# Where the four-bit weights of the last feed-forward stages are quantised: a stage of their own, or spread over rope attention

## The reference

```python
def fp4_quant_dequant(x):                       # blocks of 16 along the last dimension
    scale = max(abs(block)) / 6.0               # at least 1e-12
    idx = searchsorted(_MID, abs(block / scale))  # grid 0, .5, 1, 1.5, 2, 3, 4, 6
    return _GRID[idx] * sign(block) * scale
gate = fp4_linear(x, w_gate); y = fp4_linear(x, w_up)     # 352 x 128 each
return fp4_linear(silu(gate) * y, w_down)                 # 128 x 352
```

## Time and profile before

| | |
|---|---|
| Runs | 2240.65, 2242.89, 2244.3 us |
| Span of the profiled execution | 2239.6 us |
| Median of the runs less that span | 3.3 us |
| DVE busy | 1683.9 us, 75% |
| PE busy | 1850.4 us, 83% |
| POOL busy | 1024.6 us, 46% |

### The profile page before, as it was taken

The page is one execution under the profiler, slowest core; times in us unless marked ns, Lnnn a source line. Parts: engine busy times, 40 slices in busy tenths (PEclk is TensorE's granted clock), DMA queues, the critical chain, the costliest instruction groups (busy, mean ns, idle before and its releaser), DMA issues. The chain is left out here.

```text
span 2239.6 us, 35939 instructions
## 1 busy us (share of the span) xinstructions
PE 1850.4 (83%) x11864; PEld 1449.0 (65%) x11895; DVE 1683.9 (75%) x4329; ACT 1171.2 (52%) x2207; POOL 1024.6 (46%) x904
## 2 busy tenths in 40 slices
PE   4888877968888799957997997997994679999856
PEld 3666664746666677735775885765883467777734
DVE  7899975879899787766777775676677856777787
ACT  3777753237777565524555553334553245666332
POOL 4898951238998655502654762002662421111022
PEclk9999998979999989977998998998996879999978
DMA  3000000000000033305432431002440010000000
GB/s 123 1 1 1 1 12 1 3 1 1 1 1 1 1 105 119 100 5 124 130 117 52 133 125 59 1 0 67 135 128 6 0 49 1 2 1 2 1 0 20
DMA packets 57189, 91.49 MB, mean 41 GB/s; under 512 B 8664, under 2 KB 19736, under 8 KB 56880
## 3 DMA queue, kind: packets, MB, share of 16 engines
q1 hardware_dynamic: 57008, 89.25, 13.6%
HBM read 87.34 MB, written 1.88 MB: 40 GB/s over the span
## 5 line engine op out<-in xcount | busy, mean ns | idle before, releaser
L1041 POOL TENSOR_TENSOR unit_hid_low<-unit_hid,unit_hid_high 128x512 fp32r<-128x512 f32 x272 | 352.9, 1298 | 280.6 <-ACT unit_hid_high L1217 280.3
L800 DVE SCALAR_TENSOR_TENSOR pk_chosen<-bank,pk_least,pk_sums 128x1024 f32<-128x1024 f32 x256 | 325.6, 1274 | 44.4 <-issue 37.2
L665 ACT COPY pk_sums<-bank 128x1024 f32<-128x1024 f32 x256 | 261.2, 1021 | 123.3 <-PE bank L563 122.9
L563 PE MATMUL bank<-pk_pick,pk_sim_both 128*128 128x512 f32 x512 | 190.1, 453 | 106.6 <-DVE pk_chosen L800 106.6
L479 POOL TENSOR_TENSOR pk_chosen<-pk_chosen 128x1024 f32<-128x1024 f32 (+1 forms) x126 | 265.5, 2110 | 13.6 <-DVE pk_chosen L800 13.6
L1098 PE MATMUL bank<-unit_x_high,units_high 128*128 128x512 f32 x544 | 222.4, 409 | 19.4 <-ACT unit_gact L1210 8.3
L1099 PE MATMUL bank<-unit_x_low,units_high 128*128 128x512 f32 x544 | 218.0, 401 | 0.0
L1100 PE MATMUL bank<-unit_x_high,units_low 128*128 128x512 f32 x544 | 217.8, 400 | 0.0
L1217 ACT CAST unit_hid_high<-unit_hid 128x512 fp32r<-128x512 f32 x272 | 166.7, 613 | 55.6 <-DVE unit_hid L1364 27.8
L563 PEld LDWEIGHTS bank<-pk_pick,pk_sim_both 128*128 128x128 f32 x512 | 78.6, 192 | 165.1 <-DVE pk_chosen L800 128.5
L1210 ACT ACTIVATE unit_gact<-bank,units_small 128x512 f32<-128x512 f32 x136 | 93.7, 689 | 104.8 <-PE bank L1100 102.7
(11 more groups left out here) (404 smaller groups left out, 4456.3 us busy)
## 6 DMA issues: line engine op xcount, KB each, us to landing
unit_comb<-comb_dram SPq DMA_DIRECT2D x136, 256.0 KB, 3.2
unit_comb<-comb_dram SPq DMA_DIRECT2D x272, 128.0 KB, 3.1
raw<-in_geglu_units SPq DMA_DIRECT2D x3, 774.0 KB, 6.9
raw<-in_swiglu_units SPq DMA_DIRECT2D x3, 768.0 KB, 9.7
dh_w<-in_de_w SPq DMA_DIRECT2D x1, 1024.0 KB, 6.0
out_x<-x_res SPq DMA_DIRECT2D x1, 1024.0 KB, 5.1
raw<-in_geglu_units SPq DMA_DIRECT2D x1, 967.5 KB, 10.3
raw<-in_swiglu_units SPq DMA_DIRECT2D x1, 960.0 KB, 12.4
```

What stands on the lines that cost most here:

```text
L563: ins = nc.tensor.matmul(sums_ps[:, 2 * b + e, :], both[:, i % 2, h, :], pk.pick[:, e * PK_K // 2:(e + 1) * PK_K // 2, :].rearrange("p i j ...
L665: nc.scalar.copy(sums_sb[:, b, :].rearrange("p (e n) -> p e n", e=2), sums_ps[:, 2 * b:2 * b + 2, :]).then_inc(sums_out.sem, 1)
L800: nc.vector.scalar_tensor_tensor(chosen[:, h, :].rearrange("p (e n) -> p e n", e=2), sums_ps[:, 2 * b:2 * b + 2, :], least2[:, i % 2, h:h ...
L1041: nc.gpsimd.tensor_tensor(hid_low[:, i % HB, :], hid[:, i % HB, :], hid_high[:, i % HB, :].bitcast(FP32), ALU.subtract).then_inc(hidden.se ...
```

## The change

- `program`: the seven loads are issued by the first `experts_ffn` of the third layer instead of the second. `f4.quantise()` and its block are gone; `rope_attention` gets `f4`.
- Two counters are added, `f4_cleared` and `f4_scaled`.
- DVE, ahead of the loop of rope attention: `find_scales`, the scales and their reciprocals of `rows` and `cols`, interleaved (8 instructions), behind a wait for the loads and for POOL's clearing.
- POOL, ahead of its set-up: the clearing and a drain. Behind its loop: `round`, nine instructions for each of the two tensors. It does not take the step from the exponent bits; it compares the square with 4 and 16 instead.
- PE, behind its loop: `turn`, the nine transposes. ACT, behind its loop: `read_turned`, the five copies.

```diff
@@ rope_attention
+        f4.scratch(ctx)
         @block.gpsimd
         def _(pool):
+            f4.clear(pool)
+            nc.gpsimd.drain()
             nc.gpsimd.memset(zeros[:], 0.0)
...
                 nc.gpsimd.tensor_copy(xb[:], k.xnT[:, bass.ts(b, T)]).then_inc(x_in.sem, 1)
+            f4.round(pool)
...
+            f4.turn(pe)
...
+            f4.read_turned(act)
...
         def _(dve):
+            f4.find_scales(dve)
             dve.wait_ge(loaded.sem, loaded.at(80))
             with dve.Fori(0, B) as b:
...
+    f4.passed()
@@ Fp4Weights
-    def quantise(self):
...
+    def clear(self, pool):
+        self.k.nc.gpsimd.memset(self.rows[F4_CHUNKS[2][1]:P, :, 2, :], 0.0).then_inc(self.k.counter("f4_cleared").sem, 1)
+    def find_scales(self, dve):
+        dve.wait_ge(loaded.sem, loaded.at(16 * 7))
+        dve.wait_ge(cleared.sem, cleared.at(1))
+        for f, w in self.parts:
+            nc.vector.tensor_reduce(f.scale[:], blocked(w), axis=AX.X, op=ALU.max, apply_absolute_value=True)
+        nc.vector.drain()
+        for f, w in self.parts:
+            nc.vector.tensor_scalar(f.scale[:], f.scale[:], 1.0 / F4_MAX, F4_SCALE_MIN, ALU.mult, ALU.max)
+        nc.vector.drain()
+        for f, w in self.parts:
+            nc.vector.reciprocal(f.inv[:], f.scale[:])
+        nc.vector.drain()
+        for f, w in self.parts:
+            nc.vector.tensor_scalar_mul(f.inv[:], f.inv[:], F4_TIES_DOWN).then_inc(scaled.sem, 1)
+    def round(self, pool):
+        pool.wait_ge(scaled.sem, scaled.at(2))
+        for f, w in self.parts:
+            near, step = f.near[:], f.step[:].bitcast(FP32)
+            nc.gpsimd.tensor_tensor(blocked(near), blocked(w), over(f.inv[:]), ALU.mult)
+            nc.gpsimd.drain()
+            nc.gpsimd.tensor_tensor(w, near, near, ALU.mult)
+            nc.gpsimd.drain()
+            nc.gpsimd.tensor_scalar(step, w, 4.0, F4_ROUND, ALU.is_ge, ALU.mult)
+            nc.gpsimd.tensor_scalar(w, w, 16.0, 2.0 * F4_ROUND, ALU.is_ge, ALU.mult)
+            nc.gpsimd.drain()
+            nc.gpsimd.tensor_tensor(step, step, w, ALU.add)
+            nc.gpsimd.drain()
+            nc.gpsimd.tensor_scalar(step, step, F4_ROUND, None, ALU.add)
+            nc.gpsimd.drain()
+            nc.gpsimd.tensor_tensor(near, near, step, ALU.add)
+            nc.gpsimd.drain()
+            nc.gpsimd.tensor_tensor(near, near, step, ALU.subtract)
+            nc.gpsimd.drain()
+            nc.gpsimd.tensor_tensor(blocked(w), blocked(near), over(f.scale[:]), ALU.mult).then_inc(rounded.sem, 1)
+    def turn(self, pe):
+        pe.wait_ge(rounded.sem, rounded.at(2))
...
+    def read_turned(self, act):
+        act.wait_ge(turned.sem, turned.at(1))
...
@@ program
-                experts_ffn(k, ew)
-                rope_attention(k, a)
-                experts_ffn(k, ew, f4.load)
-        f4.quantise()
+                experts_ffn(k, ew, f4.load)
+                rope_attention(k, a, f4)
+                experts_ffn(k, ew)
```

More of the change, by code:

```diff
@@ L68 @@
     comb_in_0 comb_in_1 comb_in_2 comb_in_3 comb_in_4
-    loaded set_up f4_loaded f4_rounded f4_turned dh_loaded
+    loaded set_up f4_loaded f4_cleared f4_scaled f4_rounded f4_turned dh_loaded
     x_in
@@ L2058, with rope_attention @@
 ROPE_BASE = 10000.0
-def rope_attention(k, a):
+def rope_attention(k, a, f4):
     nc = k.nc
@@ new lines, in scratch @@
+    def scratch(self, ctx):
+        self.f_rows, self.f_cols = Fp4Scratch(self.k, ctx, 6 * P), Fp4Scratch(self.k, ctx, F4_I)
+        self.parts = ((self.f_rows, self.rows[:].rearrange("p i c d -> p (i c d)")), (self.f_cols, self.cols[:]))
+    def clear(self, pool):
+        self.k.nc.gpsimd.memset(self.rows[F4_CHUNKS[2][1]:P, :, 2, :], 0.0).then_inc(self.k.counter("f4_cleared").sem, 1)
+    def find_scales(self, dve):
+        nc, loaded, cleared, scaled = self.k.nc, self.loaded, self.k.counter("f4_cleared"), self.k.counter("f4_scaled")
+        dve.wait_ge(loaded.sem, loaded.at(16 * 7))
[11 more added lines that the diff above has]
+            nc.vector.tensor_scalar_mul(f.inv[:], f.inv[:], F4_TIES_DOWN).then_inc(scaled.sem, 1)
@@ new lines, in round @@
+    def round(self, pool):
+        nc, scaled, rounded = self.k.nc, self.k.counter("f4_scaled"), self.k.counter("f4_rounded")
+        pool.wait_ge(scaled.sem, scaled.at(2))
[17 more added lines that the diff above has]
+            nc.gpsimd.tensor_tensor(blocked(w), blocked(near), over(f.scale[:]), ALU.mult).then_inc(rounded.sem, 1)
@@ new lines, in turn @@
+    def turn(self, pe):
+        k, nc, rounded, turned = self.k, self.k.nc, self.k.counter("f4_rounded"), self.k.counter("f4_turned")
+        pe.wait_ge(rounded.sem, rounded.at(2))
+        for i in range(2):
+            for c, (at, n) in enumerate(F4_CHUNKS):
+                nc.tensor.transpose(k.bank[i][:, at:at + n], self.rows[0:n, i, c, :], k.ident[0:n, 0:n])
+        for c, (at, n) in enumerate(F4_CHUNKS):
+            ins = nc.tensor.transpose(k.bank[2][0:n, c * P:(c + 1) * P], self.cols[:, at:at + n], k.ident[:])
+        ins.then_inc(turned.sem, 1)
@@ new lines, in read_turned, with passed @@
+    def read_turned(self, act):
+        k, nc, turned = self.k, self.k.nc, self.k.counter("f4_turned")
+        act.wait_ge(turned.sem, turned.at(1))
+        for i in range(2):
+            nc.scalar.copy(self.up[:, i, :], k.bank[i][:, 0:F4_I])
+        for c, (at, n) in enumerate(F4_CHUNKS):
+            nc.scalar.copy(self.down[0:n, c, :], k.bank[2][0:n, c * P:(c + 1) * P])
+    def passed(self):
+        self.loaded.passed(16 * 7)
+        for name, n in (("f4_cleared", 1), ("f4_scaled", 2), ("f4_rounded", 2), ("f4_turned", 1)):
+            self.k.counter(name).passed(n)
```

## The result

| | before | after | ratio, 95% interval |
|---|---|---|---|
| Median of the runs | 2241.77 us (4 runs, 2240.58 to 2244.3) | 2228.3 us (4 runs, 2227.78 to 2232.16) | 0.9943 (0.9928 to 0.9958) |
| The same comparison again, E11 | 2243.59 us (11 runs, 2235.78 to 2247.05) | 2231.41 us (6 runs, 2230.54 to 2233.92) | 0.995 (0.9936 to 0.9965) |

A forecast was written before the change was run, and what follows sets the result against it. No engine was taken as full; the serial quantising stage lay wholly on the path. -16.1 (stage) + 1.2 (rotation) + 3.9 (one-element holds) + 2.0 (tail) = -9.0 us, to 2233.9 us, range 2228.5 to 2239.0.

The forecast's parts named there:

- The stage goes: Between second expert stage and the next: the quantising stage's 16.4 us shrink to a 0.32 us passage, -16.1 us.
- Scales and loads: Scales ahead of VectorE's rope attention loop, loads in the first expert stage: both covered, 0 us, scales with 1.2 to spare.
- Rounding on GpSimd: Behind GpSimd's rope attention set-up: lasts 20.5 us, off the path with over 100 us of cover.
- upper price: GpSimd's tensor-scalars priced like plain two-input instructions, 2.39 ns per column, so the rounding lasts 25 us.
- the 5.9 at which the change would have lost: Slower case: GpSimd's compares at 5.9 ns per column make VectorE's waits lose the remaining 9.0 us; chance 0.03.
- The last rotation: First pass of rope attention: VectorE's last rotation is held by GpSimd's first product, +1.2 us, or 0.
- The one-element L2285: VectorE's one-element scaling before each exponential is held by GpSimd's reads: 5.9 us, +3.9 after absorbing, ends 0 and 11.
- The first rival: One-element instructions are free; only the last rotation and one or two joins are held: -12.2 us, 2230.7; chance 0.28.
- Transposes and copies: At the end of rope attention, uncovered: nine transposes and five copies add 2.0 us, bounds 1.3 and 3.0.
- no slower than before: The stage after the removed quantising stage starts earlier and keeps its length, TensorE's clock having been at 0.50 already: 0.

The follow-up runs named there:

- E11: The changed kernel itself once more, measured beside two later runs: 2231.41 us, 0.995 against the kernel before.
- E7: The kernel before with only the seven loads moved from the second to the first expert stage: 2242.75 us, 1.0008.
- E4: The changed kernel with the negated row maximum made for two elements per partition in place of one: 2231.98 us, 0.9962.
- E1: The changed kernel with GpSimd's rounding left out, weights used unrounded: 2229.12 us, 0.9952 against the kernel before.
- E8: The changed kernel with the scales found three times over on VectorE ahead of its loop: 2232.99 us, 0.9964.
- E2: The changed kernel with 24 GpSimd memsets, which only write, in place of the rounding: 2230.61 us, 0.9954.
- E5: The changed kernel with GpSimd waiting for the first pass's six rotations before it starts rounding: 2231.07 us, 0.9954.
- E9: The changed kernel with 24 drains on VectorE ahead of the scales, shifting its loop's code: 2228.99 us, 0.9937.
- E6: The changed kernel with the transposes and copies moved into the first four-bit feed-forward stage: 2232.6 us, 0.9961.

## Why the prediction was right, and where it was not

*The stage goes:* right, -16.02 for -16.1.

*Scales and loads:* right for VectorE and for SyncE, both free (2.23 us of cover left for 1.2 forecast; E7 1.0008 with 0.9992 to 1.0024). What the prediction put at 0 on GpSimd, its clearing and the drain, costs TensorE 0.4 us where the sines land early (1.81 us in after, 1.38 in E7).

*Rounding on GpSimd:* mis-sized. It lasts from 1391.49 to 1420.53, 29.0 us, for 20.5 forecast and 25 at the upper price. The tensor-scalars with two operations take 2.79/768 = 3.63 ns per column and that with one 2.15/768 = 2.80; my bounds were 1.02 and 2.39. The two rows that I bracketed them with, a copy and a two-input product, were not a bracket. Over 100 us of cover kept the rounding itself off the path, and 3.63 is far from the 5.9 at which the change would have lost. But the length had a consequence: 20.5 us from 1391.49 end at 1412.0, and of the four joins that were held (next but one step) three start after that, at 1413.95, 1415.36 and 1417.80. These three lost 1.5 us.

*The last rotation:* right in kind. It takes 0.69 us more, for 1.2 forecast: GpSimd's product had run for 0.65 us already when it started.

*The one-element L2285:* this step failed. "I take it that it is held as the 32-element one is" put 3.9 us into the sum; it is not held at all (153 to 156 ns in after), and E4 shows that with one element more it would be. The first rival had this right. What it had too small was its other term: one or two joins of two inputs, 0.7 us. Four were held in GpSimd's 29 us: three of maxima and one of sums (L2305), a line which the prediction did not name; they lost 1.9 us. Together with the rotation 2.6, of which the stretch shows 2.4 (E1 takes all of it away).

*Transposes and copies:* right, +1.8 for +2.0.

*What no step had:* the passage between the passes, +2.1 us. It is neither the rounding (E1 keeps it), nor the work of the scales (E8 trebles it and the passage shrinks to 2.26), nor GpSimd's other work (E2 keeps it as well). Nor is it TensorE's clock (1.00 in E5). Inserting 24 drains (E9) removes it. What is shown is that the wait is VectorE's own, falls at the loop's branch back, goes with the instruction packets on q14 (two, one or none in the passage for 5.0, 2.9 and 2.26 us), and depends on where the loop's code lies. By which rule it depends on that is not shown.

*Around the block:* the second expert stage is 1.5 us shorter in after (171.7) than before (173.2), and what follows L202 is 1.8 longer (529.7 for 527.9). Both repeat, and nearly cancel. The first goes with a single dip of TensorE's clock to 0.50, 3.4 us long, some 35 us into the stage. Before, E1, E2, E6, E7 and E8 have it and take 172.8 to 173.3 us; the other seven runs do not and take 171.3 to 171.7. Here are windows of before, in the dip, and of after, at the same place (length, then busy time of PE, PEld, DVE, ACT and POOL, granted clock, DMA share, GB/s):

```profile
1558.30:1561.70 3.40, 3.40 (x10) 2.62 (x9) 3.08 (x7) 2.06 (x4) 2.35 (x3) 0.51 0.72 171
```

```profile
1561.60:1565.00 3.40, 3.40 (x16) 2.72 (x15) 3.08 (x7) 2.23 (x4) 2.35 (x3) 1.00 0.71 160
```

What decides on the dip is open. The 1.8 us lie in the first `fp4_ffn` as a whole: from L202 to the next stage's L202 it is 93.4 us before and 93.3 in E7, 95.3 in after and E11, and 94.5 to 95.7 in all eleven runs without the quantising stage, while what follows is 434.2 to 434.7 everywhere. TensorE's granted clock over that stage fell a little, 0.75 to 0.71 (windows of before and then of after):

```profile
1711.60:1806.00 94.40, 50.67 (x224) 36.43 (x224) 77.95 (x164) 27.05 (x71) 33.44 (x25) 0.75 0.04 12
```

```profile
1697.30:1793.00 95.70, 52.78 (x224) 38.68 (x224) 77.07 (x161) 26.92 (x71) 33.39 (x25) 0.71 0.03 9
```

I expected that stage "no slower than before", and it is 1.9 us slower. That step failed too. Its 224 matmuls take 2.1 us more of TensorE in it, and its clock is at 0.50 for 54 of its 95 us in after and for 46 of 93 before. That drops of the clock fall elsewhere once the 16 quiet microseconds ahead of the stage are gone fits this, but E1 and E2, at 0.50 for 47 us, take 94.6 to 94.7, so the time at 0.50 does not give the length by itself, and no run was made to settle it. It stays open, as do the 3 to 4 us by which the medians moved more than the account (13.5 and 12.2 for 9.5). The intervals of the two ratios reach down to 9.4 and 7.9 us, so scatter can be nearly the whole of it.

The account came out near its forecast (-9.5 for -9.0) by luck: -2.7 in the first stretch, +2.1 between the passes, and +0.3 from the second expert stage and what follows L202 offset each other.

## What to carry to other kernels

When work goes to GpSimd beside a VectorE loop, list the VectorE instructions that run beside its reads and have two SBUF inputs, and the tensor-scalars between SBUF tiles of more than one element: in these runs they were held, up to a whole GpSimd instruction each, and those that read PSUM kept their times. A join of two one-element numbers can escape as a tensor-scalar with a per-partition scalar. Move work that must run at a block's end to where the next user's engines idle anyway, and after every edit ahead of a hardware loop look at the idle time at its branch back: a wait put down to "issue" there, with packets of the kind "instruction" beside it, is worth a try with some two dozen instructions more in front of the loop.

## What the runs showed of the hardware that was not expected

- GpSimd's float tensor-scalars on SBUF are slower than its two-input products: 2.79 us with two operations and 2.15 with one, against 1.73 for a square and 1.49 with a broadcast input, all on 128x768.
- VectorE's tensor-scalar on SBUF is held by a reading GpSimd with two elements (up to 1.35 us) and not with one (0.15), nor is the one-element form with a one-element tensor as its scalar (0.21).
- Code position alone is worth 2.8 us at one branch back of VectorE's loop here: 5.01 to 5.12 us in after and E11, with two instruction packets of 8192 bytes in the passage, and 2.26 in E9, with none.
